# First mixture of batch 0 over all experts, ahead of any route, and sorted phases of three and four batches behind it

## What is computed

```python
x = x + 0.5 * ffn(norm(x))        # mixture 1: 8 experts, top 2 of each row
x = x + attention(norm(x))        # 16 heads of width 8, causal
x = x + 0.5 * ffn(norm(x))        # mixture 2: same weights, new route
x = x + 0.5 * quantized(norm(x))
x = x + gated(norm(x))
x = x + 0.5 * quantized(norm(x))
```

```python
logits = x @ router_w + router_b
topk_scores, topk_idx = top_k(logits, 2)
gates = softmax(topk_scores)
combine = sum over k of gates[k] * onehot(topk_idx[k], 8)
for e in range(8):
    h = relu(x @ W1[e] + b1[e])            # 128 -> 512
    out += (h @ W2[e] + b2[e]) * combine[..., e]
```

## Time and profile before

| | |
|---|---|
| median of 3 runs | 958.14 us (957.35 to 961.29) |
| the profiled execution | 957.2 us, span 955.4 us |
| TensorE busy | 842.1 us (88%) |
| VectorE busy | 620.0 us (65%) |
| ScalarE busy | 551.9 us (58%) |
| GpSimd busy | 658.1 us (69%) |
| mean granted clock of TensorE | 0.942 |

### The profile page before, as it was taken

How to read it: one execution, slowest core, us unless ns; L and a number is a source line. 1 busy time by engine, 2 the same in 40 slices (tenths; PEclk the granted TensorE clock), 3 DMA queues, 4 the chain that set the end, 5 groups by cost and what they waited for, 6 DMA issues and landing times.

```text
span 955.4 us, 23206 instructions
## 1 busy us (share of the span) xinstructions
PE 842.1 (88%) x7505; PEld 614.1 (64%) x7505; DVE 620.0 (65%) x1906; ACT 551.9 (58%) x1230; POOL 658.1 (69%) x843
## 2 busy tenths in 40 slices
PE   4469799989999999999999999999997998786684
PEld 3259799847665755665576556568975997354454
DVE  7620245384697888589998767973535445677675
ACT  3444345345766676665867666676663556744662
POOL 2889695998883268688625896962699984875442
PEclk9669889979999999999999999999999999886797
DMA  8777567845653524543444434434533771101001
GB/s 314 278 246 220 150 180 206 237 128 159 187 145 100 153 86 121 162 134 105 120 133 134 118 112 117 111 85 117 160 96 96 224 217 48 36 23 39 0 1 44
DMA packets 116279, 127.64 MB, mean 134 GB/s; under 512 B 14779, under 2 KB 84667, under 8 KB 116038
## 3 DMA queue, kind: packets, MB, share of 16 engines
q1 hardware_dynamic: 107974, 109.38, 39.0%
q0 software_dynamic: 8192, 16.79, 5.9%
HBM read 85.35 MB, written 40.39 MB: 132 GB/s over the span
## 4 chain that ended last, share of the span: by engine, by line
PE 55%; POOL 16%; DVE 13%; ACT 7%; issue 6%; DMA 2%; SPq 0%; POOLq 0%; DVEq 0%; ACTq 0%
PE bank L793 50%; POOL z_scratch L1689 7%; PE bank L805 5%; POOL small L1680 5%; DVE sm_m L1313 3%; ACT P L1564 2%; POOL yg L1702 1%; ACT zb L1477 1%; POOL sm_f L1664 1%; ACT P L1477 1%; POOL P L1724 1%; ACT tb L1477 1%; DMA Qs<-q_scratch 1%; POOL sm_p L1664 1%; DVE xs L1254 1%
## 5 line engine op out<-in xcount | busy, mean ns | idle before, releaser
L1313 DVE TENSOR_REDUCE sm_m<-bank 128x4 f32<-128x512 f32 (+2 forms) x320 | 204.3, 682 | 46.7 <-PE bank L793 42.9
L1564 ACT ACTIVATE P<-bank 128x512 f32<-128x512 f32 x320 | 173.5, 598 | 35.6 <-PE bank L793 35.2
L793 PE MATMUL bank<-w2r,hb 128*128 x1360 | 187.9, 282 | 0.0
L793 PE MATMUL bank<-zt,wt 128*128 128x128 f32 x1360 | 183.4, 285 | 1.8 <-ACT P L1564 0.7
L793 PEld LDWEIGHTS bank<-zt,wt 128*128 128x128 f32 x1360 | 167.9, 198 | 13.7 <-issue 5.5
L1724 POOL TENSOR_SCALAR_AFFINE_SELECT P<-P 128x256 f32<-128x256 f32 (+1 forms) x320 | 114.1, 373 | 84.9 <-ACT P L1564 80.8
L1689 POOL DMA_INDIRECT z_scratch<-zb,pos x128 | 133.7, 1045 | 51.2 <-DVE pos L1236 26.2
L793 PEld LDWEIGHTS bank<-w2r,hb 128*128 128x128 f32 x1360 | 165.6, 192 | 2.0 <-issue 0.3
L1523 ACT ACTIVATE hb<-bank 128x512 f32<-128x512 f32 x170 | 100.6, 595 | 91.3 <-PE bank L793 91.3
L1702 POOL DMA_INDIRECT yg<-y_scratch,pos x128 | 132.2, 1033 | 23.9 <-issue 19.8
L1680 POOL TENSOR_TENSOR small<-small 128x4 f32<-128x4 f32 x137 | 144.3, 1053 | 3.2
(11 more groups left out here) (219 smaller groups left out, 1401.4 us busy)
## 6 DMA issues: line engine op xcount, KB each, us to landing
wt<-w_scratch SPq DMA_DIRECT2D x170, 256.0 KB
zin<-z_scratch SPq DMA_DIRECT2D x82, 128.0 KB
y_scratch<-yt SPq DMA_DIRECT2D x82, 128.0 KB
q_scratch<-qpart SPq DMA_DIRECT2D x48, 128.0 KB
k_scratch<-kpart SPq DMA_DIRECT2D x48, 128.0 KB
Ks<-k_scratch SPq DMA_DIRECT2D x64, 96.0 KB
Qs<-q_scratch SPq DMA_DIRECT2D x64, 96.0 KB
z_scratch<-P SPq DMA_DIRECT2D x6, 512.0 KB, 7.7
```

The source lines that it names most:

```text
L793: return e.matmul(o, lhs, rhs, start=start, stop=stop, **kw)
L1313: e.tensor_reduce(to, of, AX.X, ALU.max, negate=True).then_inc(*d_max.step(i, f"m{s_}"))
L1564: e.activation(P[:, (2 * i + s_) % PR, :], shared("scor", i, 0, s_), ACT.Exp, scale=SCALE).then_inc(*a_sc.step(i, f"e{s_}"))
```

## The change

Batch 0 leaves the sorted phases in mixture 1. `DENSE` holds that unit. It is computed with all eight experts, with raw `W1` and the raw router (`b1c` brings `b1` by columns, `router_b` and `router_w`):

- `prep` of unit 0 normalizes all 128 columns into `ob`, transposes into a tile `z0t`, takes the raw router, adds its bias on VectorE, and makes `shares`: for each row the gate of each expert, zero for six.
- `dhid`, 32 steps: one product of an expert's 128 hidden columns with all 512 rows, relu with bias on ScalarE into one of two sets of four tiles (`hidden`).
- `dres`, 32 steps, four for each expert: one product for the bias, four for the output of one tile; VectorE adds the result to `x` with the expert's share.

The other 15 units make five phases: mixture 1 of batches 1 to 3 and of 4 to 7, then mixture 2 as before; 155 blocks. `split` moves to VectorE: `wrow` loads new rows `wr` (the last row repeated, 2 MB in all) into eight tiles, and VectorE subtracts them from `P`. The second weights `w2r`, one load of 2 MB before, come in eight with `sload`. SyncE's queue then holds the second fill of `z_scratch` and the late loads ahead of the writes to `w_scratch`.

```diff
-ORDER = [of(1, 0, 1), of(1, 2, 3, 4), of(1, 5, 6, 7), of(2, 0, 1), of(2, 2, 3, 4), of(2, 5, 6, 7)]
+ORDER = [of(1, 1, 2, 3), of(1, 4, 5, 6, 7), of(2, 0, 1), of(2, 2, 3, 4), of(2, 5, 6, 7)]
+DENSE = of(1, 0)
...
-    "split": ("P0.97+0.2 A0.6+0.15 S0.52+4",
-            [(0, 1)], 1),
+    "wrow": ("S0.47+7",
             [], 1),
+    "split": ("D0.6+0.15 S0.52+4",
+            [], 1),
...
+    "dhid": ("P0.88+0.2 A0.5+0.2",
+            [(0, 1)], 1),
+    "dres": ("P1+0.2 D0.4+0.15",
+            [(0, 1)], 1),
...
+    if stage == "dhid":
+        return [("prep", 0, 5), ("sload", u // NC, 0), ("dres", 4 * (u // NC - 2) + 3, 0)] if k == 0 else []
+    if stage == "dres":
+        return [[("dhid", NC * (u // 4) + 3, 1), ("bias", 0, 3), ("sload", u // 4, 0)], [("prep", 0, 9)]][k]
...
-    counts = {"begin": 1, "first": 1, "xload": NB - 2, "zero": 1, "fill": 1, "late": 1, "sload": NE, "split": NE, "wquant": 1, "prep": 2 * NB, "route": PHASES, "scat": NTILE,
-              "bias": 1,
+    counts = {"begin": 1, "wrow": NE, "zero": 1, "fill": 1, "first": 1, "xload": NB - 2, "late": 1, "sload": NE, "split": NE, "wquant": 1, "prep": 2 * NB, "route": PHASES, "scat": NTILE,
+              "bias": 1, "dhid": NC * NE, "dres": 4 * NE,
...
+            def sload(n):
+                e.dma_start(P[:, n, :], a["w1"][n]).then_inc(l_raw[n], 16)
+                e.dma_start(w2r[:, n, :], a["w2"][:, n, :]).then_inc(l_w2[n], 16)
+                yield
+
+            def wrow(n):
+                e.dma_start(last_row(n), a["wr"][n]).then_inc(l_wr, 16)
+                yield
...
+            def dhid(i):
+                e_, c = divmod(i, NC)
+                o = take("dhid", i, 0, a_dhid.at(i, "h"))
+                w.wait_ge(*a_prep.at(0, "zt"))
+                w.wait_ge(l_raw[e_], 16)
+                mm(o, P[:, e_, 128 * c:128 * c + 128], z0t[:, :], True, True).then_inc(*t_dhid.step(i, "h"))
+                yield
+
+            def dres(i):
+                e_, j = divmod(i, 4)
+                o = take("dres", i, 0, d_dres.at(i, "x"))
...
+                mm(o[:, 0:128], ones[:, :], bias[:, 128 * e_:128 * e_ + 128], True, False, skip_group_check=True)
+                for c in range(NC):
+                    t = mm(o[:, 0:128], hidden(e_, c)[:, j, :], w2r[:, e_, 128 * c:128 * c + 128], False, c == NC - 1,
+                           skip_group_check=True)
+                t.then_inc(*t_dres.step(i, "y"))
+                yield
...
+            def split(n):
+                w.wait_ge(l_wr, 16 * NE)
+                w.wait_ge(l_raw[n], 16)
+                e.tensor_tensor(last_row(n), P[:, n, :], last_row(n), ALU.subtract).then_inc(*d_split.step(n, "w"))
+                yield
+
+            def dres(i):
...
+                e.scalar_tensor_tensor(out=x, in0=shared("dres", i, 0)[:, 0:128], scalar=shares[:, 2, j, e_:e_ + 1], in1=x, op0=ALU.mult,
+                                       op1=ALU.add).then_inc(*d_dres.step(i, "x"))
+                yield
...
+            def dhid(i):
+                e_, c = divmod(i, NC)
+                w.wait_ge(*t_dhid.at(i, "h"))
...
+                e.activation(flat(hidden(e_, c)[:, :, :]), shared("dhid", i, 0), ACT.Relu, bias=b1c[:, i:i + 1]).then_inc(*a_dhid.step(i, "h"))
+                yield
```

More of the change, by code:

```diff
@@ L54 @@
     PHASE.append(Phase(_f))
-OF_UNIT = [f for f in range(PHASES) for _ in range(PHASE[f].units)]
+OF_UNIT = [None] * len(DENSE) + [f for f in range(PHASES) for _ in range(PHASE[f].units)]
 OF_TILE = [f for f in range(PHASES) for _ in range(PHASE[f].tiles)]
@@ L60, with first_tile @@
 SLOTS = KB * SB
+def first_tile(m, b):
+    return 4 * (UNIT[m, b] - len(DENSE))
 def pieces_of(f, start, end):
```

165 lines of the change are left out of this document (107 added, 58 removed), and 13 rows, old and new, of the table STAGES.

## The result

| | before | after |
|---|---|---|
| median, lowest to highest | 959.06 us (957.35 to 961.29) | 980.43 us (977.51 to 980.99) |
| ratio, 95% interval | 1 | 1.0223 (1.0205 to 1.0241) |
| profiled execution, its span | 957.2, 955.4 | 977.5, 975.8 |
| first sorted block | 60.03 | 92.40 |
| last output projection | 658.92 | 678.23 |

The change makes the kernel 21 us slower. The prediction said 964, with 949 to 975 as its range. The direction was right; the size was not, and the time lies above the range.

The account below looks back on a forecast made before the run. TensorE, busy 842 of 955.4 us, was taken as the bound; early work pays only from the first 60 us and the gap at 104. 957.2 + 27.0 - 26.7 - 4.8 + 11 = 963.7, said as 964; range 949 to 975.

Parts of the forecast that it names:

- first sorted block: Start: the first block of sorted tokens moves from 60.0 to 87 us, +27.0, with bounds 21 and 34.
- TensorE's work, first block to last output projection: Middle: 17 sorted blocks fewer at 2.005 us each, against 7.4 us of remaining dense work: -26.7 us.
- the gap at 104 to 116 goes: Behind the first sorted phase: TensorE's 4.8 us wait vanishes, since last dense work and batch 0's projections lie there: -4.8.
- idle of the stretch between second and third output projection: Middle: without block work VectorE becomes the bound, the stretch takes 63 us and TensorE waits 14 instead of 2.9: +11.
- the end: After the last output projection: two more blocks, hidden in TensorE's 7.8 us wait for the last phase's rows: no cost.
- a gap that moved behind the first sorted phase: Sign of a wrong forecast: 32 scatters, most with a square root between them, must end before the second phase loads.
- the time of the route's positions: Start: positions of the three-batch route ready at 35 us, chosen between 22.3 and 40.
- The stretch without blocks: Between second and third output projection: near 63 us, with TensorE below 80% and VectorE above 90%.
- The rule on VectorE and GpSimd: Start: VectorE's two-SBUF-input subtractions contend with GpSimd's scatters, adding up to 5.4 us to the GpSimd chain; sum unchanged.
- work counts alone: Rival, 25%, faster: VectorE doesn't bound the stretch between second and third output projection, which takes under 52 us; total 952.7.
- The start is late: Rival, 17%, slower: loads and subtractions come 10 us later, first sorted block at 97, total 974.
- The ramp of the attention goes as well: Rival, 8%: batch 0 is ready early, so TensorE's 4.2 us of idling in 200 to 240 vanish; total 960.

Follow-up runs that it names:

- e6b: Changed kernel with the six fills of Ks moved to the second route's block table, run a second time: 978.13 us, beside 984.18 for the unchanged changed kernel.
- e1: Changed kernel with the eight subtractions of `split` moved, on VectorE alone, behind the eighth dense addition: 976.97 us, ratio 1.0199 to the kernel before.
- e11: Changed kernel with 32 row maxima of the scores, in the stretch without blocks, taken over 64 of 512 columns: 1001.13 us, ratio 1.0427 to the kernel before.
- e7: Changed kernel with subtractions behind the first dense additions, fills of Ks early, no pauses between the second sorted phase's 32 scatters: 1008.14 us, ratio 1.0495.
- e6: Changed kernel with the six fills of Ks moved to the second route's block table, first run: 995.05 us, ratio 1.0357 to the kernel before.
- c1: The changed kernel run again without any edit, as a control: 984.18 us, ratio 1.0270 to the kernel before.
- c2: The changed kernel run once more without any edit, as a control in another group: 999.26 us, ratio 1.0415 to the kernel before.
- e2: Changed kernel with the last four wide dense products and outputs moved ahead of the first sorted block: 981.65 us, ratio 1.0238 to the kernel before.
- e3: Changed kernel with the sorted phases of the kernel before, batch 0 still dense, planned anew: 972.67 us, ratio 1.0157 to the kernel before.
- e9b: Changed kernel without the work of experts 4 to 7 in the dense mixture, run a second time: 995.81 us, ratio 1.0349 to the kernel before.

## Why the prediction was wrong

By its own sum, against the span, in its order:

| step | forecast | measured |
|---|---|---|
| first sorted block | +27.0 (87) | +32.4 (92.4) |
| TensorE's work, first block to last output projection | -26.7 | -25.2 |
| the gap at 104 to 116 goes (measured: all idle time from the first block to the first output projection) | -4.8 | +0.7 |
| idle of the stretch between second and third output projection | +11 | +12.1 |
| other idle of the middle | 0 | -0.6 |
| the end | 0 | +1.1 |
| sum | +6.5 | +20.5 |

Two steps failed, by 5.5 and 5.4 of the 14 us.

- **The gap that did not go** (5.5 us). I wrote that the last dense work and batch 0's projections would lie in it. Two waits stand in its place. From 176 to 183 TensorE waited 5.3 us, 3.6 of them for the second phase's first rows: part of the old gap, moved. My sign "a gap that moved behind the first sorted phase" came true, by the trace for SyncE's order as much as for the 32 scatters; no run tells the two apart. And the projection brought a wait of its own, 4.95 us in the middle of the first phase. I counted the moved work and not the order in which ScalarE's and VectorE's queues hold it. e6b shows the cause of 2.9 of these: six fills of 0.91 us on VectorE.
- **The first block** was 5.4 us late. What failed is the time of the route's positions, which I had chosen between two values: 39.7, not 35. Five dense outputs stood ahead of the route's own products in TensorE's order, at a granted clock of 0.76. The rest of that chain held. 11 wide products and 7 outputs were done when TensorE stood, as forecast; from the positions to the first addition it was 7.9 us (8 forecast), and from TensorE's next product to the first block 44.4 (44 forecast, 2 of them for the clock; from 48 to 54 it was 0.59, an estimated 2.5 us lost). The idle time was 18.0 us against 17. e1 won back 4.0 us by moving the subtractions; no run moved the dense outputs behind the route's products, so that the positions come earlier was not tested.
- **The stretch without blocks** came at 70.1 us, not 63, with TensorE under 80% and VectorE at 85%, not above 90. That the 11 us came out as 12.1 is luck, for the reason given fell: "it becomes the bound" was tested in e11, where VectorE lost 13.6 us and the stretch 0.6. TensorE's own 49 us were 55, much of it at half clock. The neighbouring stretches soaked up nothing.
- **TensorE's work in the middle** was right to 1.5 us, and the count of blocks with it. In all 869.9 us were busy instead of 862. The start has 49.8 us more than before, the middle 25.2 less, the end 3.2 more for its two blocks. My terms did not agree among themselves: 70 us in the start, 26.7 less in the middle and two more blocks at the end make 865, not 862.
- **The rule on VectorE and GpSimd** was overdrawn. The Trainium skill (SBUF — State Buffer, "Who interferes with whom") let me add up to 5.4 us to the scatters. The starts at 39.99 and 48.36 span five distances of 1.26 and a square root of about 1.05, 7.4 us; they took 8.4. It cost 1 us, on a chain that did not bind: a sign that the rule holds in part, and no test of it.

Of the rivals, "work counts alone" fell with the stretch (70, where it wanted under 52). "The start is late" named the right place and a wrong cause: no load was late, and the block came at 92 instead of its 97. "The ramp of the attention goes as well" was right in what I held against it: batch 0's projections do not stand behind all 31 blocks, its first score product came at 170.2 instead of 183.1, and in 200 to 240 TensorE was busy for 39.8 us instead of 35.8. That gain is in the +0.7 too; the two waits above ate it up. The steps I priced were additions and removals; what I missed, in both the gap and the half clock, is what a wait does to the queues beside it.

## What to carry to other kernels

Work moved into an idle stretch is free only up to the idle time that disappears: here 27.8 us were added in all, and 7.4 us of idle time went. Before moving a stage forward, list everything its steps issue on each in-order queue, fills and other one-time work included, and ask what stands behind each: the projection of a batch that is ready early blocked rows that were ready too. And a stretch in which two engines are 85% busy need not be bound by either: shorten one as an experiment before calling it the bound.

## What was not expected

- The changed kernel took 980, 984 or 999 us depending on the group, where the kernel before varied by 2. For about 16 us SyncE, ScalarE and VectorE stood while GpSimd scattered every 1.26 us. It starts only behind 54 us, when the first ten scatters have been issued. That it needs close scatters is likely from e7 against e6 (19 us more in one group), not shown for the first phase. What decides between the groups is open.
- A wait of 4.4 us cost about 2 us more behind it: twice 1.02 us for the pair of products at 47.99, and a granted clock of 0.59 until 54. c1, c2, e2 and e6b show the same wait and the same 2.07 or 2.08 us. In e1, with 1.6 us of waiting, the clock stayed at 1.00. But e3 waited 1.64 us ahead of its pair at 36.21, and the pair took 2.08 us, with 0.71 granted until 42. So the length of that one wait does not decide, and a shorter wait does not promise the full clock.
- Taking work out can save less than its price: e9b's TensorE had 16 wide products and 16 outputs less, and lost 12.9 us of busy time instead of 28, the granted clock of its start being 0.74.
